# Streaming 64 columns instead of 128 in the TensorE slots of a two-way scan in which one half of the samples takes part

## The chip, the cores and the metric

The kernel runs on one core of a Trainium2 chip. The metric is the device time of that core in microseconds, the median of 3 runs. It runs in float32 throughout.

## The reference

The input `x` has 4 samples of 512 channels, 32 rows and 48 columns. Each sample is first normalised over groups of 16 channels. Then a recurrence goes over the 48 columns, forwards and afterwards backwards over what the forward pass left; the input is added at the end.

```
Wc = conv_w[:, :, 0, 4]                        # 512 x 512, the middle tap of nine
def step(prev, x_i):
    y = einsum('oc,nch->noh', Wc, prev) + conv_b
    y = where(y >= 0, y, prelu_a * y)
    cur = y + x_i
    return (cur, cur)
_, fwd_rest = scan(step, x[0], x[1:])          # over the 48 columns
_, bwd_rest = scan(step, fl[-1], fl[:-1], reverse=True)
x = x + (fwd and bwd result of group_norm(x))
```

Each step needs the one before it: 47 steps forwards and 47 backwards, in each a 512x512 matrix times 512 channels by (samples x 32 rows).

## The kernel before

**Two halves, a few steps apart.** Samples 0 and 1 are half A, samples 2 and 3 are half B. A half has 64 columns (`COLS`: 2 samples x 32 rows) for every one of the 48 positions. Half A starts first, half B follows `SKEW` = 5 steps later, so that its load and its statistics can lie beside the first steps of A. A *slot* is one step of whatever halves take part. There are 99 slots (`LAST`), numbered j: slots 0 to 4 with half A alone (phase "lead"), slots 5 to 93 with both halves ("both forward", "turn", "both backward"), and slots 94 to 98 with half B alone ("drain").

**TensorE, in a slot.** The 512x512 product is 16 units, 4 blocks k of input channels by 4 blocks o of output channels, in the order of the table `UNITS` (L19): tile o=0 is complete with the 9th unit, tile 1 with the 11th, tile 2 with the 13th, tile 3 with the 16th. Each unit is one matmul instruction at L266. Its weights are a 128x128 block of `w_t`. Its moving operand comes from `state`: with both halves `moving` (L138) calls `state_tile`, which takes 2 x 64 columns, one from each half. With one half alone `moving` makes an access pattern with a step of 0 in front, `[0, 2]`, so that the same 64 columns are streamed twice and the matmul writes 128 columns of its PSUM bank. Even slots use banks 0 to 3, odd slots banks 4 to 7.

**What waits for what.** Before the first unit of each k, TensorE waits on `state_ready` for the four-fold count that says that block k of the slot before is final (L265). With the last unit of a tile it raises `tile_done`. ScalarE (L304 to L308) waits for tile o and reads the columns `c` of the halves that take part: twice a Relu, into `above` and, with the sign turned, into `below`. VectorE (or GpSimd, below) adds `above` into `state` (L442), then VectorE adds `below` times the negative slope (L449) and raises `state_ready`; the order within a slot is the table `ORDER` (L22): part 0, whole 0, part 1, part 2, whole 1, whole 2, part 3, whole 3. In the backward phases VectorE then adds the result to the input, in place in `xio` (L461, `add_input`).

**The lead (slots 0 to 4).** GpSimd does the first add (L551), VectorE the second (L476). Between its slots VectorE computes statistics of half B (L363, `stats_b`). ScalarE does those of two of the eight channel blocks of half B (L327 and L330, `pieces`), after its own part of slots 0 to 3. When all are there, VectorE computes means and reciprocal roots (`group_stats`), normalises position 0 of half B (L400, L401) and raises `norm_b`. TensorE, which has meanwhile issued 16 matmuls on the identity (`KEEP_UP`, L275), waits for `norm_b` and then begins slot 5. Earlier, before the last transpose of the weights, it issues 24 of these (`WARM_UP`, L247).

**The drain and the store.** The queue of SyncE stores half A (two transfers of 3 MB) after `out_ready` 1, which VectorE raises at the end of slot 93, and half B (two more) after `out_ready` 2, at the end of slot 98 (L232 to L238). The transfers of half A run while half B is still being computed in the drain.

The lines that the change touches, and those that wait on them:

```
mm = nc.tensor.matmul(psum[:, 4 * par + o, 0:2 * COLS], w_t[:, k, o * P:(o + 1) * P],
                      xs[k], start=k == 0, stop=k == 3)
if k == 3:
    mm.then_inc(tile_done, 1)
```

Of the kernel before, what the change touches and what calls it, by code (L numbers as in the profile page):

```python
# [10 lines left out]
P = 128  # L11
# [19 lines left out]
def scan_program(nc, x, conv_w, conv_b, prelu_a, out):  # L31
# [3 lines left out]
    COLS = NG * H  # L35
# [13 lines left out]
    with ExitStack() as ctx:  # L49
        def sb(name, shape, dt=F32):  # L50
            return ctx.enter_context(nc.sbuf_tensor(name, shape, dt))
# [7 lines left out]
        state = sb("state", [P, 2, W, KT, COLS])  # L59
        w_t = sb("w_t", [P, KT, C])  # L60
# [21 lines left out]
        psum = ctx.enter_context(nc.psum_tensor("psum", [P, 8, 512], F32))  # L82
# [25 lines left out]
        SROW, XROW = 2 * W * FEAT, 2 * KT * COLS * W  # L108
# [9 lines left out]
        def w_raw_block(o, k):  # L118
            t, room = (xio, XHALF) if o < 2 else (state, SHALF)
            base = room + (o % 2) * C * TAPS + k * P * TAPS + MID  # L120
            return bass.AP(t, base, [[SROW, P], [TAPS, P]])
# [5 lines left out]
        def cols(mode):  # L127
            return {"A": slice(0, COLS), "B": slice(COLS, 2 * COLS), "AB": slice(0, 2 * COLS)}[mode]

        def halves(mode, wa, wb, base, step, whole, gap):  # L130

            if mode == "A":
                return wa * step + base, []
            if mode == "B":
                return wb * step + whole + base, []
            return wa * step + base, [[whole + gap * step, 2]]

        def moving(eng, mode, wa, wb, gap, k):  # L138


            if mode == "AB":
                return state_tile(eng, mode, wa, wb, gap, k)
            off, _ = halves(mode, wa, wb, k * COLS, FEAT, SHALF, gap)
            return bass.AP(state, reg(eng, off, 0, SROW - COLS), [[SROW, P], [0, 2], [1, COLS]])

        def reach(half):
            return half[0][0] if half else 0
# [2 lines left out]
        def state_tile(eng, mode, wa, wb, gap, o):  # L150
            off, half = halves(mode, wa, wb, o * COLS, FEAT, SHALF, gap)
            return bass.AP(state, reg(eng, off, 0, SROW - COLS - reach(half)), [[SROW, P]] + half + [[1, COLS]])
# [26 lines left out]
        def positions(j, phase, back=0):  # L179

            fa, ba = j + (1 - back), j * -1 + (STEPS - 1 + back)
            if phase == "lead":
                return "A", fa, None, 0
            if phase == "both forward":
                return "AB", fa, None, -SKEW
            if phase == "turn":
                return "AB", ba, None, fa - SKEW - ba
            if phase == "both backward":
                return "AB", ba, None, SKEW
            return "B", None, ba + SKEW, 0  # L190

        def loop(eng, first, last, body):

            n = (last - first) // UNROLL
            if n > 1:
                with eng.Fori(0, n) as turn:
                    for u in range(UNROLL):
                        body(turn * UNROLL + (first + u), (first + u) % 2)
                first += UNROLL * n
            for j in range(first, last):  # L200
                body(j, j % 2)

        def reg(eng, value, low, high):

            return value if isinstance(value, int) else eng.snap(value, min_val=low, max_val=high)

        def ready(eng, ap):

            eng.lower_ap(ap)
            return ap  # L210

        @block.sync
        def _(sp):
            def load_x(n):
                for t in range(KT):
                    sp.dma_start(xio[:, n // NG, t, (n % NG) * H:(n % NG + 1) * H, :],  # L216
                                 x[n, t * P:(t + 1) * P, :, :]).then_inc(x_loaded[n][t], 16)

            for n in range(NG):
                load_x(n)  # L220
            w_rows = conv_w.rearrange("(o p) i a b -> o p (i a b)", p=P)
            for o in range(KT):
                sp.dma_start(w_raw(o), w_rows[o]).then_inc(w_loaded[o], 16)  # L223
            sp.wait_ge(w_turned, 2)
            for n in range(NG, N):
                load_x(n)

            def store(n):
                sp.dma_start(out[n].rearrange("(t p) h w -> p t h w", p=P),
                             xio[:, n // NG, :, (n % NG) * H:(n % NG + 1) * H, :]).then_inc(stored, 16)  # L230

            sp.wait_ge(out_ready, 1)  # L232
            for n in range(NG):
                store(n)
            sp.wait_ge(out_ready, 2)
            for n in range(NG, N):
                store(n)
            sp.wait_ge(stored, 16 * N)  # L238

        @block.tensor  # L240
        def _(pe):

            pe.wait_ge(ident_done, 2)
            for o in range(KT):
                if o == KT - 1:
                    for _ in range(WARM_UP):
                        nc.tensor.matmul(psum[:, KT, 0:P], ident[:, :], ident[:, :], start=True, stop=True)  # L247
                pe.wait_ge(w_loaded[o], 16)
                for k in range(KT):
                    t = nc.tensor.transpose(psum[:, o, k * P:(k + 1) * P], w_raw_block(o, k), ident[:, :])  # L250
                t.then_inc(w_turned, 1)
            pe.wait_ge(w_ready, KT)
            pe.wait_ge(norm_a, 1)

            def slot(phase):
                def body(j, par):
                    mode, wa, wb, gap = positions(j, phase, back=1)
                    xs = [ready(pe, moving(pe, mode, wa, wb, gap, k)) for k in range(KT)]
                    before = [reg(pe, j * 4 + (k - 3), 1, 4 * LAST) for k in range(KT)]
                    seen = set()  # L260
                    for k, o in UNITS:
                        if k not in seen:
                            seen.add(k)
                            if not (isinstance(j, int) and j == 0):
                                pe.wait_ge(state_ready, before[k])  # L265
                        mm = nc.tensor.matmul(psum[:, 4 * par + o, 0:2 * COLS], w_t[:, k, o * P:(o + 1) * P],  # L266
                                              xs[k], start=k == 0, stop=k == 3)
                        if k == 3:
                            mm.then_inc(tile_done, 1)
                return body  # L270

            slot("lead")(0, 0)
            loop(pe, 1, SKEW, slot("lead"))
            for _ in range(KEEP_UP):
                nc.tensor.matmul(psum[:, 4 * (SKEW % 2), 0:P], ident[:, :], ident[:, :], start=True, stop=True)  # L275
            pe.wait_ge(norm_b, 1)
            slot("both forward")(SKEW, SKEW % 2)
            loop(pe, SKEW + 1, FWD + 1, slot("both forward"))
            for j in range(FWD + 1, FWD + SKEW + 1):
                slot("turn")(j, j % 2)  # L280
            loop(pe, FWD + SKEW + 1, STEPS, slot("both backward"))
            loop(pe, STEPS, LAST, slot("drain"))
# [298 lines left out]
```

## Time and profile before

| | |
|---|---|
| device time, 3 runs | 429.28, 428.53, 429.04 us; median 429.04 |
| span of the profiled execution | 426.3 us |
| median less that span | 2.7 us |
| TensorE (PE) busy | 370.0 us, 87% |
| VectorE (DVE) busy | 329.7 us, 77% |
| ScalarE (ACT) busy | 227.1 us, 53% |
| moved to and from HBM | 34.73 MB |

For the profiled execution the page gives the span, from its first to its last instruction, and no device time of its own; the span is set beside the median here. A row of the page's groups gives the line, the engine, the operation, output<-input, the count, the busy time and the mean of one. PEld is TensorE's weight load. TensorE's records come in twos: the program has 16 matmuls in a slot, the trace 32 records, and 99 slots give the 3168 of L266. The end of a matmul record is modelled, so the spacing of the starts tells more than the length of a record.

### The profile page before, as it was taken

Reading aid. Unit: us, or ns where it says so; the run is one execution under the profiler, and the core shown is the slowest. Engines: PE = TensorE matmul, PEld = TensorE weight load, DVE = VectorE, ACT = ScalarE, POOL = GpSimd, SP = SyncE. Lnnn points to the kernel's source line nnn. Section 1 sums busy time; section 2 is a strip of 40 time slices with the busy share of each in tenths; the row PEclk is TensorE's granted clock in tenths of the full one; section 3 lists DMA queues with packets and bytes.
Section 4 is the critical chain, followed back from the end, with each engine's and each line's share of the span. In section 5 each row is a group of like instructions: output and inputs, shape, how many; then the busy total and the mean of one; then the engine's idle time right before and its main releaser. Section 6 shows DMA issues by size and latency. Waiting matters only on the chain.

```text
span 426.3 us, 10441 instructions
## 1 busy us (share of the span) xinstructions
PE 370.0 (87%) x3264; PEld 367.7 (86%) x3264; DVE 329.7 (77%) x976; ACT 227.1 (53%) x831; POOL 9.2 (2%) x28
## 2 busy tenths in 40 slices
PE   0015989999999999999999999999999999999920
PEld 0015889999999999999999999999999999999920
DVE  3989588999866666666667899999999999999620
ACT  1001594655566666666666666666666666665510
POOL 0000131000000000000000000000000000000000
PEclk9999999999999999999999999999999999999985
DMA  7999920000000000000000000000000000001989
GB/s 262 434 426 420 415 112 2 1 0 0 1 0 0 0 0 0 0 0 0 0 0 2 2 0 0 0 0 0 0 0 0 0 0 0 0 0 43 413 348 379
DMA packets 5674, 34.73 MB, mean 81 GB/s; under 512 B 1056, under 2 KB 1056, under 8 KB 5152
## 3 DMA queue, kind: packets, MB, share of 16 engines
q1 hardware_dynamic: 4992, 34.60, 19.7%
q10 hardware_dynamic: 672, 0.00, 0.1%
q8 instruction: 5, 0.08, 0.1%
q14 instruction: 5, 0.04, 0.0%
HBM read 22.02 MB, written 12.58 MB: 81 GB/s over the span
## 4 chain that ended last, share of the span: by engine, by line
PE 82%; DMA 7%; ACT 3%; DVE 2%; SPq 1%; issue 1%; POOL 0%; DVEq 0%; POOLq 0%
PE psum L266 80%; DMA state<-in_conv_w 7%; PE psum L247 1%; SPq L216 1%; ACT state L327 1%; ACT above L306 1%; ACT below L308 1%; ACT state L330 1%; DVE bstat L363 0%; PE psum L250 0%; SPq L223 0%; DVE chan L366 0%; ACT scaled L333 0%; POOL inv_root L542 0%; DVE state L400 0%
## 5 line engine op out<-in xcount | busy, mean ns | idle before, releaser
L266 PE MATMUL psum<-state,w_t 128*128 (+1 forms) x3168 | 356.2, 275 | 2.9 <-DVE state L476 2.2
L266 PEld LDWEIGHTS psum<-state,w_t 128*128 128x128 f32 x3168 | 354.9, 192 | 4.3 <-DVE state L476 2.0
L306 ACT ACTIVATE above<-psum,bias 128x128 f32<-128x128 f32 (+1 forms) x396 | 145.2, 367 | 139.1 <-PE psum L266 138.4
L442 DVE TENSOR_TENSOR state<-above,state 128x128 f32 (+3 forms) x376 | 106.3, 285 | 54.3 <-ACT above L306 53.1
L308 ACT ACTIVATE below<-psum,neg_bias 128x128 f32<-128x128 f32 (+1 forms) x396 | 145.4, 367 | 0.0
L449 DVE SCALAR_TENSOR_TENSOR state<-below,neg_slope,state 128x128 f32 (+3 forms) x376 | 121.9, 345 | 6.9
L461 DVE TENSOR_TENSOR xio<-xio,state (+2 forms) x54 | 52.8, 978 | 1.8
L391 DVE TENSOR_SCALAR state<-xio,gstat 128x384 f32<-128x384 f32 (+2 forms) x72 | 35.9, 572 | 0.0
L363 DVE BATCH_NORM_STATS2 bstat<-xio 128x6 f32<-128x512 f32 x42 | 26.1, 680 | 8.1 <-DMA xio<-in_x 8.1
L250 PE MATMUL psum<-ident,xio 128*128 128x128 f32 x8 | 2.2, 433 | 30.5 <-DMA xio<-in_conv_w 30.5
L250 PEld LDWEIGHTS psum<-ident,xio 128*128 128x128 f32 x8 | 1.4, 216 | 30.9 <-issue 25.6
L295 ACT COPY w_t<-psum 128x512 f32<-128x512 f32 x4 | 2.3, 586 | 33.8 <-PE psum L250 33.8
L476 DVE SCALAR_TENSOR_TENSOR state<-below,neg_slope,state 128x64 f32<-128x64 f32 x20 | 5.6, 302 | 5.3 <-POOL state L551 5.3
L551 POOL TENSOR_TENSOR state<-above,state 128x64 f32<-128x64 f32 x20 | 7.1, 363 | 32.4 <-ACT above L306 31.7
L247 PEld LDWEIGHTS psum<-ident 128*128 128x128 f32 x48 | 6.6, 225 | 0.0
L247 PE MATMUL psum<-ident 128*128 128x128 f32 x48 | 6.6, 305 | 0.0
L250 PE MATMUL psum<-ident,state 128*128 128x128 f32 x8 | 1.7, 355 | 4.4 <-DMA state<-in_conv_w 4.4
L250 PEld LDWEIGHTS psum<-ident,state 128*128 128x128 f32 x8 | 1.3, 204 | 4.8 <-DMA state<-in_conv_w 4.8
L330 ACT ACTIVATE state<-xio,chan 128x512 f32<-128x512 f32 x6 | 4.4, 738 | 0.1
L327 ACT ACTIVATE state<-xio 128x512 f32<-128x512 f32 x6 | 3.8, 637 | 0.1
L275 PE MATMUL psum<-ident 128*128 128x128 f32 x32 | 3.7, 275 | 0.0
L275 PEld LDWEIGHTS psum<-ident 128*128 128x128 f32 x32 | 3.7, 192 | 0.0
(28 smaller groups left out, 14.6 us busy)
## 6 DMA issues: line engine op xcount, KB each, us to landing
xio<-in_x SPq DMA_DIRECT2D x16, 768.0 KB, 13.6
out_y<-xio SPq DMA_DIRECT2D x4, 3072.0 KB, 13.5
xio<-in_conv_w SPq DMA_DIRECT2D x2, 2304.0 KB, 22.9
state<-in_conv_w SPq DMA_DIRECT2D x2, 2304.0 KB, 33.0
bias<-in_conv_b ACTq DMA_DIRECT2D x1, 2.0 KB, 5.9
slope<-in_prelu_a ACTq DMA_DIRECT2D x1, 0.5 KB, 8.0
```

Source lines behind the costliest of these rows:

```text
L247: nc.tensor.matmul(psum[:, KT, 0:P], ident[:, :], ident[:, :], start=True, stop=True)
L266: mm = nc.tensor.matmul(psum[:, 4 * par + o, 0:2 * COLS], w_t[:, k, o * P:(o + 1) * P], xs[k], start=k == 0, stop=k == 3)
L275: nc.tensor.matmul(psum[:, 4 * (SKEW % 2), 0:P], ident[:, :], ident[:, :], start=True, stop=True)
L306: nc.scalar.activation(above[:, par, o, c], z, ACT.Relu, bias=bias[:, o:o + 1], scale=1.0).then_inc(above_done, 1)
L308: nc.scalar.activation(below[:, par, o, c], z, ACT.Relu, bias=neg_bias[:, o:o + 1], scale=-1.0).then_inc(below_done, 1)
L327: last = nc.scalar.activation(junk, x_piece(1, n, ct, s), ACT.Identity, accum_out=piece_sum[:, 0, s:s + 1])
L330: last = nc.scalar.activation(junk, x_piece(1, n, ct, s), ACT.Square, scale=-1.0, bias=chan[:, 0, b:b + 1], accum_out=piece_sum[:, 1, s:s ...
L363: return nc.vector.bn_stats(bstat[:, b, s, :], x_piece(g, b % NG, b // NG, s))
L391: return nc.vector.tensor_scalar(norm_out(g, b, w0, w1), norm_in(g, b, w0, w1), gstat[:, g, 0, b:b + 1], gstat[:, g, 1, b:b + 1], ALU.subt ...
L442: nc.vector.tensor_tensor(sts[o], split(mode, above[:, par, o, c]), sts[o], ALU.add).then_inc(part_done, 1)
L449: nc.vector.scalar_tensor_tensor(sts[o], split(mode, below[:, par, o, c]), neg_slope[:, 0:1], sts[o], ALU.mult, ALU.add).then_inc(state_re ...
L461: return nc.vector.tensor_tensor(place, place, result, ALU.add)
```

## The change

In slots with one half, `moving` returns an access pattern of 64 columns without the leading repeat, and the matmul writes only the columns of its PSUM bank that belong to the half that takes part, 0 to 63 for A and 64 to 127 for B, as `cols` gives them. With both halves nothing differs (`cols("AB")` is 0 to 127). It is 160 of the 1584 matmul instructions: 80 in slots 0 to 4 and 80 in slots 94 to 98.

```
@@ moving
             if mode == "AB":
                 return state_tile(eng, mode, wa, wb, gap, k)
             off, _ = halves(mode, wa, wb, k * COLS, FEAT, SHALF, gap)
-            return bass.AP(state, reg(eng, off, 0, SROW - COLS), [[SROW, P], [0, 2], [1, COLS]])
+            return bass.AP(state, reg(eng, off, 0, SROW - COLS), [[SROW, P], [1, COLS]])
@@ slot, TensorE
-                        mm = nc.tensor.matmul(psum[:, 4 * par + o, 0:2 * COLS], w_t[:, k, o * P:(o + 1) * P],
+                        mm = nc.tensor.matmul(psum[:, 4 * par + o, cols(mode)], w_t[:, k, o * P:(o + 1) * P],
                                               xs[k], start=k == 0, stop=k == 3)
```

Nothing is moved. On TensorE, slot 0 and the start of the loop over slots 1 to 4 (in the rows, 128x64 is the shape that the matmul writes; ISA and REGISTER_ALU rows compute addresses and counts):

```order
-L266 MATMUL psum<-state,w_t 128x128 x16
+L266 MATMUL psum<-state,w_t 128x64 x16
 L196 UNCONDITIONAL_BRANCH
 L196 ISA
 L209 ISA x2
-L266 MATMUL psum<-state,w_t 128x128 x4
+L266 MATMUL psum<-state,w_t 128x64 x4
 L265 REGISTER_ALU
```

The shape of what is written differs, and no instruction is added, dropped or put elsewhere; the other engines' instructions are the same, in the same order.

## Rows read from the trace of the kernel before

**Rows 1.** The page: engines' busy time, and the chain by engine and line.
```profile
PE 370.0 (87%) x3264; PEld 367.7 (86%) x3264; DVE 329.7 (77%) x976; ACT 227.1 (53%) x831; POOL 9.2 (2%) x28
PE 82%; DMA 7%; ACT 3%; DVE 2%; SPq 1%; issue 1%; POOL 0%; DVEq 0%; POOLq 0%
```

**Rows 2.** The chain that ended last, in time: start us, us, what.
```profile
45.71 3.85 PE psum L266 x32
49.59 0.31 ACT above L306
...
61.24 0.31 ACT above L306
...
62.87 0.42 POOL state L551
...
70.07 0.29 DVE state L476
70.36 0.14 issue
70.49 337.27 PE psum L266 x3008
...
408.73 0.60 DVE xio L461
```

**Rows 3.** Timeline of TensorE, 44 to 75 us: start, length, engine, line, operation, count.
```profile
45.71 7.47 PE L266 MATMUL psum<-state,w_t 128*128 128x128 f32 x64 [0.68 <-ACT w_t L295]
53.67 3.84 PE L266 MATMUL psum<-state,w_t 128*128 x32 [0.49 <-DVE state L476]
...
62.33 3.84 PE L266 MATMUL psum<-state,w_t 128*128 x32 [0.46 <-DVE state L476]
66.01 3.74 PE L275 MATMUL psum<-ident 128*128 128x128 f32 x32
```

**Rows 4.** Timeline of the lead, 45 to 75 us, ScalarE and VectorE.
```profile
48.08 0.31 ACT L306 ACTIVATE above<-psum,bias 128x64 f32<-128x64 f32 x1 [2.42 <-PE psum L266]
48.29 0.31 ACT L308 ACTIVATE below<-psum,neg_bias 128x64 f32<-128x64 f32 x1
...
63.31 0.28 DVE L476 SCALAR_TENSOR_TENSOR state<-below,neg_slope,state 128x64 f32<-128x64 f32 x1 [0.22 <-POOL state L551]
...
64.04 1.81 DVE L363 BATCH_NORM_STATS2 bstat<-xio 128x6 f32<-128x512 f32 x3
...
72.78 0.37 ACT L306 ACTIVATE above<-psum,bias 128x128 f32<-128x128 f32 x1 [5.42 <-PE psum L266]
```

**Rows 5.** Timeline of the drain, 385 to 412 us, all engines.
```profile
392.28 0.23 DVE L442 TENSOR_TENSOR state<-above,state 128x64 f32 x1
...
399.08 0.31 ACT L306 ACTIVATE above<-psum,bias 128x64 f32<-128x64 f32 x1 [1.49 <-PE psum L266]
399.43 0.23 DVE L442 TENSOR_TENSOR state<-above,state 128x64 f32 x1 [0.79 <-ACT above L306]
...
401.26 0.28 DVE L449 SCALAR_TENSOR_TENSOR state<-below,neg_slope,state 128x64 f32 x1
401.58 0.63 DVE L461 TENSOR_TENSOR xio<-xio,state  x1
402.65 0.31 ACT L306 ACTIVATE above<-psum,bias 128x64 f32<-128x64 f32 x1 [1.49 <-PE psum L266]
```

**Rows 6.** By stretch: PE, PEld, DVE, ACT, POOL busy (x), PEclk, DMA share, GB/s.
```profile
57.00:61.00 4.00, 3.48 (x31) 3.29 (x30) 3.21 (x8) 3.90 (x17) 1.46 (x4) 1.00 0.02 6
400.00:407.00 7.00, 7.00 (x65) 7.00 (x64) 4.65 (x18) 3.72 (x17) 0.00 (x0) 1.00 1.02 417
408.00:409.00 1.00, 0.00 (x0) 0.00 (x0) 0.86 (x4) 0.31 (x2) 0.00 (x0) 1.00 0.44 178
409.00:410.00 1.00, 0.00 (x0) 0.00 (x0) 0.33 (x1) 0.00 (x0) 0.00 (x0) 1.00 0.07 31
410.00:411.00 1.00, 0.00 (x0) 0.00 (x0) 0.00 (x0) 0.00 (x0) 0.00 (x0) 1.00 0.81 326
412.00:413.00 1.00, 0.00 (x0) 0.00 (x0) 0.00 (x0) 0.00 (x0) 0.00 (x0) 0.63 1.04 424
413.00:424.00 11.00, 0.00 (x0) 0.00 (x0) 0.00 (x0) 0.00 (x0) 0.00 (x0) 0.50 1.01 416
```

**Rows 7.** TensorE's weight loads and matmuls, a quarter of a microsecond from 37.30.
```profile
37.09 0.69 PE L250 MATMUL psum<-ident,state 128*128 128x128 f32 x2 [4.37 <-DMA state<-in_conv_w]
37.18 0.41 PEld L250 LDWEIGHTS psum<-ident,state 128*128 128x128 f32 x2
```

**Rows 8.** Two stretches of 3.00 us around 40 us, columns as in rows 6.
```profile
37.10:40.10 3.00, 3.00 (x14) 3.00 (x15) 3.00 (x6) 0.59 (x1) 0.00 (x0) 1.00 0.98 418
40.50:43.50 3.00, 3.00 (x29) 3.00 (x28) 1.81 (x4) 0.00 (x0) 0.00 (x0) 1.00 0.94 387
```

More of the change, by code:

```diff
@@ L143, in moving @@
             off, _ = halves(mode, wa, wb, k * COLS, FEAT, SHALF, gap)
-            return bass.AP(state, reg(eng, off, 0, SROW - COLS), [[SROW, P], [0, 2], [1, COLS]])
+            return bass.AP(state, reg(eng, off, 0, SROW - COLS), [[SROW, P], [1, COLS]])
         def reach(half):
@@ L265, in body @@
                                 pe.wait_ge(state_ready, before[k])
-                        mm = nc.tensor.matmul(psum[:, 4 * par + o, 0:2 * COLS], w_t[:, k, o * P:(o + 1) * P],
+                        mm = nc.tensor.matmul(psum[:, 4 * par + o, cols(mode)], w_t[:, k, o * P:(o + 1) * P],
                                               xs[k], start=k == 0, stop=k == 3)
```

## The prediction

> **What bounds the kernel now.** I read the page first, then the chain, then the timelines of the two stretches that the change touches. TensorE is busy 87% of the span and holds 82% of the chain [rows 1]. In time the chain says more [rows 2]: TensorE from 70.49 us for 337.27 us without a break. That is 3008 records, 112.1 ns each, and a slot of 32 records takes 3.59 us. The slots that the change touches lie at both ends of this piece. The lead, slots 0 to 4, runs from 45.71 to 70.49 us and its chain goes over ScalarE, GpSimd and VectorE; the drain, slots 94 to 98, lies in the last 17 us of the piece, and there TensorE sets the pace. Between them nothing is changed, so the middle should move as a block, earlier or later by what the lead gives.
>
> After the last computation (408.73 + 0.60 = 409.33 us [rows 2]) the span goes on for another 17.0 us with stores alone. The drain therefore has two clients: the computation of half B, and the transfers of half A that run beside it.
>
> **The new duration of a matmul.** A record takes 112 ns for 128 columns. Two passes of 128 columns at 2.4 GHz are 107 ns, so I read a record as two passes and little else. The trace has no 64-column matmul. Bounds: from below one half, 56 ns; from above no change, 112 ns. What could keep it from halving is the load of the 128x128 weights, once per record, which becomes no smaller. It is hidden now. How long it takes can be read where the engine was slow. At 37 us, after an idle time of over 4 us, 14 records took 3 us, 214 ns each, and from 40.5 us on 29 took 3 us, 103 ns by the count [rows 8]; I read this as 1.2 GHz and then 2.4 GHz, though the clock column shows 1.00 in both. In the slow stretch the first matmul started at 37.09 us and the second weight load at 37.18 [rows 7], with nothing before it but the first load; so a load takes about 0.1 us at the slow clock. If it follows the array's clock it is about 50 ns at the fast one, less than the 56 of the stream. I take 60 ns, near the lower bound, since the row on the load speaks for it. A slot's TensorE work goes from 3.59 to 1.92 us.
>
> The Trainium skill speaks against this ("TensorE: Matmul & The Clock Gate", section on LDWEIGHTS): it gives the load as the number of weight columns over 1.2 GHz, which is 107 ns for 128 columns, and elsewhere says that the fast load does not apply to float32. By that rule the sum below would be about -0.8 instead of -2.95. Rows 7 agree with its figure at the slow clock, and no row shows it at the fast one.
>
> **Term 1, the lead.** ScalarE is the bound there. It receives the first tile of slot 0 at 48.08 us after waiting 2.42 us [rows 4] and its next idle time in the timeline is the one before slot 5, at 72.78 us [rows 4]: its eight Relus of a slot follow at 0.21 us each (48.08 to 48.29 [rows 4]), then come the statistics of half B, then the next slot. Four later slots of TensorE begin when VectorE has released them and end long before ScalarE comes for them, so halving those saves nothing: their cover is ScalarE's statistics, about 2.6 (4.3 less eight times 0.21) of the 4.3 us from slot to slot. What the chain does hold is slot 0: TensorE 45.71 + 3.85, then ScalarE's `above` of the last tile at 49.59 [rows 2]. TensorE ends slot 0 at 49.56; records there come at 115 ns (3.85 less the 0.28 of the last, over 31). With 60 ns tile 0, 18 records in, is complete 18 x 0.055 = 0.99 us earlier, at 47.09 on ScalarE; the last tile would be 32 x 0.055 = 1.8 us earlier. But ScalarE needs six Relus at 0.21 us before it, so its start is 47.09 + 1.26 = 48.35 rather than 49.59: **-1.24 us**, call it -1.25. Everything behind follows, ScalarE's statistics, the `above` of slot 3 at 61.24, GpSimd at 62.87, VectorE to 70.07, and `norm_b` [rows 2]. The loads of half B are not late for it: from 57 us on they take 2% of the transfer time [rows 6], and VectorE's last statistics, at 64.04 us [rows 4], would begin at 62.8.
>
> At the end of the lead TensorE has less to do. Slot 4 now starts at 62.33 and the 32 records of `KEEP_UP` at 66.01 for 3.74 us [rows 3], which leaves a pause of 0.75 us before slot 5 at 70.49. Afterwards slot 4 would start at about 61.1 and end by 63.4 (it waits for VectorE's last tile, 63.31 + 0.28 less 1.25 [rows 4], before its last 8 units). `KEEP_UP` ends at 67.1 and slot 5 begins at 69.2: a pause of 2.1 us. I count it as nothing, if the clock holds.
>
> **Term 2, the drain.** A slot takes 3.57 us: ScalarE starts tile 0 at 399.08 and at 402.65, each time after 1.49 us of waiting for TensorE [rows 5]. VectorE waits 0.79 us of it. Its own work begins at 399.43 and ends at 401.58 + 0.63 = 402.21, 2.78 us. With 1.92 us on TensorE the cycle is closed by VectorE: from its first add T, the last block is final at T + 2.11 (401.26 + 0.28 less 399.43), TensorE then needs 0.06 us to notice, one unit of 0.12 and about 0.22 for the tail of a matmul and the signal, and ScalarE's `above` comes 0.35 us ahead of VectorE's add (399.08 to 399.43). That is 2.86 us, so a slot takes about 2.8 to 2.9. The first add of the drain, at 392.28, cannot come earlier than the add of slot 93 ahead of it on VectorE allows. Four periods follow: 4 x 0.7 = 2.8 us less until the last output is ready.
>
> The stores cap this. The transfers of half A end in the 408 us slice, those of half B begin in the 410 us slice. In the three slices together 178 + 31 + 326 = 535 of 3 x 417 were moved [rows 6]; what is missing is 1.72 us at full rate. As soon as `out_ready` 2 comes 1.72 us earlier, the second pair of stores is queued behind the first without a gap and the rest of the gain only makes it wait longer. **-1.7 us**, and 1.1 us of the drain's 2.8 are lost to the queue. Any slot time up to 3.14 us gives the same.
>
> **Sum.** -1.25 - 1.7 = -2.95 us: span 426.3 to 423.35, and with the 2.7 us between span and median, 429.04 to 426.1 us. About 0.9 us, 0.2%, is what a measurement here can tell from no change.
>
> **Rivals.** (a) *The weight load binds* at 107 ns, clock-independent. The lead gives 32 x 0.005 = 0.16 us, the drain 4 x (3.57 - 32 x 0.107) = 0.6: 428.2 us. If matmuls don't get shorter at all, 429.0. For it: nothing in the trace shows a load at the fast clock. Against: rows 7. Chance 0.17, which also holds the case that the change does nothing.
>
> (b) *The clock falls once and the gain of the lead is given back.* TensorE would be busy about 2 of every 4.3 us in the lead instead of 3.84, and pause 2.1 us before slot 5. The trace shows the granted clock at 1.00 with pauses of up to 0.75 us, and falling to 0.63 and then 0.50 in the 412 and 413 us slices, over 4 us after the last matmul [rows 2, 6]. Pauses like those to come are not in it. In the lead itself a slow matmul costs nothing (it is back at the old 112 ns or so). In slot 5 it does: the slow stretch at 37 us lasted 3 us [rows 8], and 3 us at half speed lose 1.5. Lead -1.25 + 1.5 = +0.25, drain -1.7 or, if the clock falls there too, -0.6: 427.6 to 428.7 us. Chance 0.18. The Trainium skill bears this out in its section on HAM oscillation in the same page: bursts of matmuls with waits between them can lose the clock again and again. No row here shows that happening.
>
> (c) *The clock stays low into slot 5 and past it: slower.* The place is again the hand-over from `KEEP_UP` to slot 5. A slot of both halves at the slow clock takes 32 x 0.214 = 6.8 us instead of 3.6, and loses 3.2. Then the lead is +2.0 and, with the drain at the slow clock at -0.6, the result +1.4: 430.4 us. It decides from 2 x (1.25 + 0.6) = 3.7 us of slow work in slots 5 and later if the drain gives 0.6, from 5.9 if it gives 1.7. For it: after the change the lead has the least TensorE activity of the program. Against: a slot of both halves is uninterrupted work, and the one rise in the trace took 3 us of it. Chance 0.14.
>
> **How the numbers follow.** The forecast, 426.1, has 0.51; its own range, with the pitch between 56 and 80 ns (at 80 the lead gives 1.0), is 425.5 to 426.7. Rival (a) 0.17, (b) 0.18, (c) 0.14. Faster by over 0.2%: the forecast, most of (b), and little of (a), 0.51 + 0.12 + 0.05 = 0.68. Within 0.2%: the rest of (a) and (b) and a little of (c), 0.19. Slower: 0.13. The range goes from 425.2 to 429.6, which leaves out most of (c) and a tail below.
>
> **What would show it.** Right: records of L266 in the lead at 56 to 65 ns; ScalarE's first tile at 47.1 and slot 5 at 69.2 us; a drain period of 2.8 to 2.9 with VectorE hardly idle; no dip of the transfer rate between the two pairs of stores; PEclk 1.00 throughout. Wrong: a spacing of 107 ns or more (a); a granted clock below 1.00 near 60 to 75 us, with slots of both halves above 3.6 us (b, c). If slot 5 starts early and its slots are at the old pace, but the end is not earlier, the stores were mis-read.

## The result and the profile after

The change makes the kernel slower: 436.81 us, median of 5 runs (436.32 to 442.32), against 429.09 (428.53 to 429.37) for the kernel before beside it; ratio 1.0207, 95% interval 1.0158 to 1.0256. That is +7.7 us where -2.95 was forecast. The profiled execution took 442.32 us, with a span of 440.4, the longest of the five. The ratios of this text leave out executions over 1.5% above the fastest of the same kernel, which here would hide part of the effect itself; where it matters all times are given.

The page after, the granted clock in 40 slices and the chain, against rows 1:

```profile
PE 386.2 (88%) x3264; PEld 384.6 (87%) x3264; DVE 329.7 (75%) x976; ACT 228.7 (52%) x831; POOL 8.6 (2%) x28
PEclk9999755799999999999999999999999999999975
PE 87%; DMA 7%; SPq 1%; DVE 0%; ACT 0%; issue 0%
```

Half the columns in 160 matmuls, and TensorE is busy 16 us longer. The clock row has a dip at slices 5 to 8 that the kernel before hadn't. The chain in time, against rows 2:

```profile
46.85 32.12 PE psum L266 x160
78.97 5.85 PE psum L275 x32
84.83 336.98 PE psum L266 x3008
421.80 0.02 issue
421.82 0.33 ACT above L306
```

Before, the chain left TensorE after slot 0 and went over ScalarE [rows 2]. Now all 160 records of the lead and the 32 on the identity are on it without a break. From the start of slot 0 to that of slot 5 it was 70.49 - 45.71 = 24.8 us; it is 84.83 - 46.85 = 38.0. These 13.2 us are nearly all of the 14.1 us by which the spans differ. The rest, 1.1 us, is slot 0's later start: the identity matmuls before it take 7.5 us here and took 6.4 before. The change doesn't touch these, and I read the difference as one of when the clock rises: before, records came 103 ns apart from 40.5 us on [rows 8], and in the trace after only 6 fall in the microsecond from 40 us and the first 12 in the one from 43. In the traces of this case with 24 of these matmuls they take anywhere from 6.3 us (`drain_32`) to 7.8 (`drain_only`). Behind slot 5 both traces need the same (337.0 and 337.3 us).

By stretch, the clock and the count of records (columns as in rows 6):

```profile
46.85:49.35 2.50, 2.50 (x22) 2.50 (x23) 0.00 (x0) 0.18 (x1) 0.00 (x0) 1.00 1.01 415
50.00:78.00 28.00, 28.00 (x133) 28.00 (x132) 15.54 (x44) 18.59 (x67) 5.42 (x16) 0.50 0.22 92
80.00:85.00 5.00, 5.00 (x32) 5.00 (x31) 2.92 (x12) 0.00 (x0) 0.00 (x0) 0.65 0.00 0
85.00:90.00 5.00, 5.00 (x47) 5.00 (x46) 2.50 (x9) 2.19 (x8) 0.00 (x0) 1.00 0.01 3
405.40:421.50 16.10, 16.10 (x146) 16.10 (x146) 11.10 (x40) 8.97 (x38) 0.00 (x0) 1.00 0.89 363
```

Two things stand here. At the full clock a record of 64 columns comes every 114 ns in slot 0 and every 111 ns in the drain (16.10 over 145 spacings), as one of 128 columns did. And from about 50 us the granted clock is 0.50, the lower level, 1.2 GHz (by single microseconds it is 1.00 up to 49 us, 0.69 in the next and 0.50 after that, so it fell inside slot 0, in which the records follow each other without a pause). A record then takes 28.0/132 = 212 ns, 64 columns or not, a slot 32 of them, 6.8 us, more than the 4.3 that ScalarE set. The clock comes back between 80 and 85 us, when the 128-column matmuls on the identity have begun.

The drain of the kernel after keeps its pace: ScalarE's first tiles, against rows 5, are still 3.57 us apart, each after the same wait of 1.49 us.

```profile
413.12 0.31 ACT L306 ACTIVATE above<-psum,bias 128x64 f32<-128x64 f32 x1 [1.49 <-PE psum L266]
...
416.69 0.31 ACT L306 ACTIVATE above<-psum,bias 128x64 f32<-128x64 f32 x1 [1.49 <-PE psum L266]
```

### The profile page after: what moved, and what is told of

It is laid out like the page before. It is cut to its first block, busy times and chain, and to the rows that moved or that the text cites. A ratio compares the mean times of both kernels' runs of the same rounds, so it can differ in the third digit from the quotient of the medians.

```text
span 440.4 us, 10441 instructions
## 1 busy us (share of the span) xinstructions
PE 386.2 (88%) x3264; PEld 384.6 (87%) x3264; DVE 329.7 (75%) x976; ACT 228.7 (52%) x831; POOL 8.6 (2%) x28
## 4 chain that ended last, share of the span: by engine, by line
PE 87%; DMA 7%; SPq 1%; DVE 0%; ACT 0%; issue 0%
PE psum L266 84%; DMA state<-in_conv_w 7%; PE psum L247 2%; PE psum L275 1%; SPq L216 1%; PE psum L250 0%; SPq L223 0%; DVE xio L461 0%; ACT w_t L295 0%; ACT above L306 0%; DVE state L449 0%; DVE state L442 0%
## 5 line engine op out<-in xcount | busy, mean ns | idle before, releaser
L266 PE MATMUL psum<-state,w_t 128*128 (+2 forms) x3168 | 369.2, 282 | 0.7 <-ACT w_t L295 0.7
L266 PEld LDWEIGHTS psum<-state,w_t 128*128 128x128 f32 x3168 | 368.6, 198 | 1.3 <-ACT w_t L295 0.9
L247 PEld LDWEIGHTS psum<-ident 128*128 128x128 f32 x48 | 7.7, 256 | 0.0
L247 PE MATMUL psum<-ident 128*128 128x128 f32 x48 | 7.7, 337 | 0.0
L275 PE MATMUL psum<-ident 128*128 128x128 f32 x32 | 6.1, 377 | 0.0
L275 PEld LDWEIGHTS psum<-ident 128*128 128x128 f32 x32 | 6.0, 291 | 0.0
```

What stands on the lines that cost most here:

```text
L266: mm = nc.tensor.matmul(psum[:, 4 * par + o, cols(mode)], w_t[:, k, o * P:(o + 1) * P], xs[k], start=k == 0, stop=k == 3)
```

## The experiments

Two theories came from these traces. **W**: a record has a floor set by the 128 columns of its weights, so fewer moving columns save nothing. **C**: streaming half as many columns in the same time loses the full clock in the lead. The rivals are in the expectations.

### The change in one place at a time

```
 lead_only:  if mode == "A": one copy of the 64 columns, else two
 drain_only: if mode == "B": one copy of the 64 columns, else two
 lead_half (slots 0 to 4, tiles o=1 and o=3 only):
-  psum[:, 4 * par + o, 0:2 * COLS], ..., xs[k]
+  psum[:, 4 * par + o, 0:COLS if o % 2 else 2 * COLS], ..., xs[k][o % 2]
```

> 64 columns in the lead (slots 0 to 4) alone; the drain streams them twice as before. Theory C (the clock): with half the columns per record TensorE's granted clock falls in the lead, the lead is then paced by records of 214 ns, and all of the loss is here: ratio to before about 1.018, granted clock 0.50 for 20 to 34 us from about 50 us on. Rival D (the drain or something at the end has a share): clearly less than the whole change, under 1.012. Rival H (the pause before slot 5 is what loses the clock): the clock is 1.00 until about 66 us and 0.50 after it, ratio under 1.01.

Measured: 13 runs, median 437.57 us; 428.44, 428.74 and 432.9, the other ten from 435.6 to 442.6. The 29 runs of before beside it lie within 428.13 to 429.75, and so do the two fastest of this kernel. The ratio of the two medians, of all executions, is 437.57 / 428.83 = 1.020. The profiled one, a span of 440.7 us, has the clock of the change's:

```profile
50.00:80.00 30.00, 30.00 (x143) 30.00 (x143) 17.30 (x50) 19.60 (x70) 7.08 (x21) 0.50 0.21 85
80.00:84.00 4.00, 4.00 (x20) 4.00 (x20) 2.96 (x12) 0.00 (x0) 0.00 (x0) 0.50 0.00 0
84.00:88.00 4.00, 4.00 (x38) 4.00 (x37) 0.36 (x2) 0.87 (x4) 0.00 (x0) 1.00 0.01 4
```

So the lead carries the whole loss, and it is a matter of chance in each execution. Where the clock held (mean 0.984 over the execution, against 0.944 in the profiled one), nothing was gained either: 428.44 is before's own time. Rival H falls for this trace: the clock was at 0.50 from 50 us on, and the matmuls of `KEEP_UP` begin only at 78.8.

> 64 columns in the drain (slots 94 to 98) alone. Theory W (the record of a matmul has a floor that the 128 weight columns set): records stay at 112 ns, a drain slot at 3.57 us, ratio 1.000. My prediction's term 2 would be 0.996 with slots of 2.8 to 2.9 us. Under rival D the ratio is over 1.004. If the clock falls here too, slots of 6.8 us show it.

Measured: 428.99 us, ratio 0.9996 (0.9986 to 1.0007), 12 runs, none above 429.6. The whole drain at the full clock, 146 records in 16 us:

```profile
391.00:407.00 16.00, 16.00 (x146) 16.00 (x145) 11.83 (x43) 8.65 (x36) 0.00 (x0) 1.00 0.78 318
```

Theory W holds, and rival D is out.

> In the lead the output tiles 1 and 3 stream 64 columns once, the tiles 0 and 2 twice: 96 columns per record on average; the drain as before. Theory C: a clock that depends on how much is streamed falls less or not at all here, ratio between 1.000 and that of lead_only. Rival S (any 64-column matmul in the lead does it, by its shape): the same loss as lead_only.

Measured: 428.77 us, ratio 0.9998 (0.9988 to 1.0008), 10 runs, all within 428.03 to 429.56. Half of the lead's matmuls have 64 columns and the clock holds every time, so the shape in itself (rival S) does not lose it.

### What a record costs

```
 after the drain, in the kernel before:
+for m, n in [(128, 64), (128, 256), (128, 32), (128, 128), (64, 128), (64, 64), (32, 32)]:
+    for _ in range(8):
+        matmul(psum[0:m, 4, 0:n], ident[:, 0:m], w_t[:, 0, 0:n], start=True, stop=True)
```

> Before, with 7 groups of 8 matmuls (16 records each) on TensorE behind the drain, where only stores are left. Weights x moving columns: 128x64, 128x256, 128x32, 128x128, 64x128, 64x64, 32x32. Theory W (weights set the floor): 112, about 220, 112, 112, 112 (moving bound), about 60 and under 60 ns per record at the full clock. Rival F (a fixed cost per record, whatever the weights): 112 ns also for 64x64 and 32x32. Rival M (moving columns alone, what I predicted): 60 for 128x64 and 30 for 128x32.

The groups by line of this kernel (busy time, mean of one; in "128*64 128x128" the first pair is the weights, here of 64 columns, the second the 128 moving columns):

```profile
L285 PE MATMUL psum<-w_t,ident 128*128 128x256 f32 x16 | 3.7, 382 | 0.0
L285 PE MATMUL psum<-w_t,ident 128*128 128x128 f32 x16 | 2.0, 280 | 0.0
L285 PE MATMUL psum<-w_t,ident 128*64 128x128 f32 x16 | 2.0, 276 | 0.0
L285 PE MATMUL psum<-w_t,ident 128*128 128x64 f32 x16 | 1.9, 272 | 0.0
L285 PE MATMUL psum<-w_t,ident 128*128 128x32 f32 x16 | 1.9, 271 | 0.0
L285 PE MATMUL psum<-w_t,ident 128*64 128x64 f32 x16 | 1.1, 222 | 0.0
L285 PE MATMUL psum<-w_t,ident 128*32 128x32 f32 x16 | 0.7, 197 | 0.0
```

The records overlap, so the spacing is (busy less one record) over 15. With 128 weight columns it is 0.11 us at 128, 64 and 32 moving columns, and 0.22 at 256. With 64 weight columns it is 0.11 at 128 moving ones and (1.1 - 0.22)/15 = 0.06 at 64; 32 and 32 give 0.03. So in these seven pairs a float32 record's spacing goes with the larger of the two column counts. The 60 ns that I had priced exist, but only if the weights are narrowed as well; a slot would then need twice as many matmuls. The mechanism inside is my reading: loads of weights that run beside the stream of the matmul ahead. The run took 430.95 us with the extra work, one run.

### What keeps and what loses the clock

```
 lead_fill:    lead at 64 columns; behind each of its slots
+  4 x matmul(psum[:, 4 * (1 - par), 0:P], ident[:, :], ident[:, :])      KEEP_UP 16 -> 12
 lead_fill_64: the same with ident[:, 0:COLS] as the moving operand
 slot0_twice:  slot 0 and the drain twice as before, slots 1 to 4 once
 drain_32:     drain streams [[SROW, P], [1, 32]] into 32 columns (sample 3's products left out);
               the rest as before
```

> As lead_only, but behind the 16 matmuls of each slot of the lead 4 more of 128x128 on the identity (8 records, 0.9 us), and 4 fewer in front of slot 5. Theory C (the clock follows how much the array streams): the clock holds, 428.8 us, ratio 1.000, with the lead's own matmuls still at 64 columns. Rival S (64-column matmuls lose the clock by their shape) or a rival by which only the matmuls' own pace counts: 432 to 442 us as in lead_only.

Measured: median 429.39 us over 10 runs, ratio 1.0001 (0.999 to 1.0013); eight within 428.79 to 429.77, two at 436.4 and 436.6. The clock holds mostly, not always. Rival S is out here too: the lead's own matmuls are all at 64 columns.

> As lead_fill, with the fillers behind each slot of the lead at 64 columns too: TensorE has no pause in the lead, and streams 64 columns per record throughout, which is what the drain of drain_only did with the clock at 1.00. Theory P+C (it takes both, half the columns and the pauses): the clock holds in most runs, 429 us, as in the drain. Rival T (in the lead half the columns is too little in itself, and only lead_fill's 128-column fillers helped): 432 to 442 us as in lead_only.

Measured: nine of 11 runs within 429.01 to 429.83, two at 449.3; ratio 1.0002 (0.9992 to 1.0012). In the profiled run, one that held:

```profile
46.00:70.00 24.00, 23.81 (x213) 23.81 (x214) 16.79 (x48) 18.99 (x73) 6.79 (x20) 1.00 0.43 177
```

213 records in 24 us and no pause. Adding *more 64-column matmuls* to the lead mostly saves the clock. But the fillers do two things at once, they close the pauses of 0.5 us per slot and they raise what is streamed in the same time, and no run parts the two. The pauses between slots are not needed for the loss, since in the first profile of the change the clock fell before the first of them. Two runs of 11 lost it even with the fillers, and then 20 us, more than any other kernel here. So half the columns without pauses is no safe place, only a better one. The drain, with the same stream, held in all 12 runs of `drain_only`; 0 of 12 against 2 of 11 can be chance, so these runs don't show that it is safer there.

> Slot 0 and the drain stream twice as before, only slots 1 to 4 stream once. Theory C: the clock falls all the same in most runs, one slot later, and the loss is smaller, 430 to 439 us. Rival Z (slot 0, directly behind the warm-up and its pause of 0.7 us, is what decides): 428.8 us.

Measured: 4 runs, 435.68 to 437.85, median 437.1, ratio 1.0166 (1.0147 to 1.0184). In its profile the first two slots keep the old rhythm and then:

```profile
54.41 20.03 PE L269 MATMUL psum<-state,w_t 128*128 x96 [0.55 <-DVE state L480]
74.22 6.13 PE L279 MATMUL psum<-ident 128*128 128x128 f32 x32
```

Three slots in 20.0 us without a pause, 6.7 each. Rival Z falls: a full slot 0 only postpones the loss.

> In the drain only 32 of the 64 columns are streamed (the products of sample 3 are left out in slots 94 to 98); the lead as before. Theory W: records stay at 112 ns as long as the clock stays. Theory C: with a quarter of the old streaming the clock falls in the drain, slots go from 3.57 to 6.8 us from there on, and the end comes 3 to 10 us later. Rival P (what loses the clock in the lead are the pauses, and a drain without pauses never does): 3.57 us and 428.8 us.

Measured: 441.04 us (439.48 to 442.66, 4 runs), ratio 1.0295 (1.0264 to 1.0325). By stretch:

```profile
390.00:395.00 5.00, 5.00 (x47) 5.00 (x46) 4.55 (x15) 2.55 (x11) 0.00 (x0) 1.00 0.35 138
395.00:400.00 5.00, 5.00 (x27) 5.00 (x26) 2.38 (x10) 2.07 (x8) 0.00 (x0) 0.52 1.01 408
410.00:415.00 5.00, 5.00 (x25) 5.00 (x25) 2.12 (x8) 1.55 (x6) 0.00 (x0) 0.50 0.00 1
```

The drain has no pause and its records follow each other as closely as ever, and still the clock falls to 0.50 at 395 us and stays there. Rival P is out: streaming little is enough, without pauses. At the slow clock a record of 32 columns takes 5.00/24 = 208 ns, as one of 128 does, so the floor follows the array's clock.

### The pause ahead of slot 5

```
-KEEP_UP = 16
+KEEP_UP = 0        # no_keep: in the kernel before; change_no_keep: in the changed one
```

> Before, without the 16 identity matmuls ahead of slot 5: TensorE pauses 4.5 us there. Rival H of my prediction (the pause at the hand-over loses the clock): 430 to 433 us in some runs or all, with slots 5 and on at records of 214 ns for a few us. If one pause of 4.5 us does not lose it, 428.8.

Measured: 431.32 us (431.19 to 431.87, 4 runs), ratio 1.0059 (1.0042 to 1.0076). After a pause of 4.3 us the clock is low:

```profile
68.00:70.00 2.00, 0.00 (x0) 0.00 (x0) 1.10 (x6) 0.30 (x2) 1.31 (x4) 0.82 0.00 0
...
74.00:76.00 2.00, 2.00 (x11) 2.00 (x11) 0.18 (x1) 0.37 (x2) 0.00 (x0) 0.50 0.00 0
76.00:78.00 2.00, 2.00 (x20) 2.00 (x19) 1.64 (x6) 1.88 (x7) 0.00 (x0) 0.98 0.00 0
```

It came back by 76 us, under 5 us into slot 5, and the price was 2.4 us. My rival (b) is thus a real mechanism, though here with a pause of 4.3 us, twice the 2.1 that it was about, and a price of 2.4 us where I gave slot 5 1.5; what a pause of 2.1 us does was not tested. It is not what the change sets off.

> The change without the 16 identity matmuls. In the profile of the change they stand on the path with 5.9 us at the slow clock, and slot 5 begins 4.5 us after its input is ready. Theory K (they cost more than they bring once the clock is lost): 3 to 5 us less than the change in the runs with the longest loss. Theory R (only the 128-column records bring the clock back): slot 5 runs at the slow clock instead, the loss moves there, and the time stays within 2 us of the change.

Measured: 434.77 us median over 11 runs, 430.19 to 439.66. The longest runs are 442.32 - 439.66 = 2.7 us shorter than the longest of the change, a little less than theory K's 3 to 5. Its profile shows both theories at once: slot 5 begins at 75.45 us, soon after its input, and runs at the slow clock until about 79.

```profile
75.45 24.75 PE L266 MATMUL psum<-state,w_t 128*128 128x128 f32 x202 [1.17 <-DVE state L476]
76.00:78.00 2.00, 2.00 (x12) 2.00 (x11) 2.00 (x8) 0.00 (x0) 0.00 (x0) 0.50 0.00 0
```

Once the clock is lost, the 16 matmuls on the identity only stand in the way. Four of the 11 runs took 430.2 to 431.0 us, no more than `no_keep`, and three of these four have its mean clock of 0.974. I read these as runs in which the clock held through the lead and was lost only in the pause; no trace of one was kept.

### The change again, and a faster kernel

> The change itself once more, beside the others on one chip, to see how its time spreads: by theory C it depends on how long the clock stays low, so single runs at 436 and 442 us as already seen, some perhaps at 428.5 as two of lead_only; by a theory of a fixed cost all within 0.3% of 436.8.

Measured: 435.45, 435.7, 436.49 and 442.38 us; ratio 1.015 (1.0132 to 1.0169). The profile of this run shows where the shorter ones come from:

```profile
46.87 7.36 PE L266 MATMUL psum<-state,w_t 128*128 128x64 f32 x64 [0.68 <-ACT w_t L295]
54.77 3.79 PE L266 MATMUL psum<-state,w_t 128*128 x32 [0.54 <-DVE state L476]
59.12 13.58 PE L266 MATMUL psum<-state,w_t 128*128 x64 [0.57 <-DVE state L476]
72.50 5.74 PE L275 MATMUL psum<-ident 128*128 128x128 f32 x32
```

Slots 0 to 2 still have the old rhythm, and only slots 3 and 4 take 13.6 us. In the first profile the clock fell during slot 0. The time depends on when in the lead it falls; none of the nine runs of the change escaped, and two of the 13 of `lead_only` did. The lead is the same in both, and in `change_no_keep`, where by the times about four of 11 escaped, so I take that for chance.

```
-WARM_UP = 24
+WARM_UP = 16       # in the kernel before
```

> Before, with 16 instead of 24 identity matmuls ahead of the last transposes (L247). In the profile of before they take 6.4 us on the chain, while the last block of weights has landed by about 42 us. If the clock holds, slot 0 begins up to 1.8 us earlier and ScalarE's chain with it: 427 to 428 us. If fewer of them leave the clock low at slot 0, the lead is paced by records of 214 ns for a while: 430 to 436.

Measured: 427.33 us (426.97 to 427.91, 4 runs), ratio 0.995 (0.9935 to 0.9965), faster than both kernels. The chain in its trace, against rows 2:

```profile
38.36 5.41 PE psum L247 x32
43.77 0.47 PE psum L250 x4
44.26 0.59 ACT w_t L295
44.90 3.85 PE psum L266 x32
```

Slot 0 begins at 44.90 instead of 45.71 us and slot 5 at 69.67 instead of 70.49. The two traces so explain 0.8 of the 2.1 us between the medians (429.44 beside it); the trace of before (span 426.3) is among its shortest, and the executions beside `warm_16` have spans up to 427.8. Fewer of these matmuls still bring the full clock before slot 0, whose 32 records take 3.85 us in both traces. The lead's 128-column records then hold it.

## Why the prediction was wrong

**The new duration of a matmul: the step that failed.** I took 60 ns for a 64-column record, between bounds of 56 and 112; it measures 111 to 114, the upper bound. The reading that led me there was that of rows 7: the second weight load is shown 0.09 us after the first, at the slow clock, so I halved it for the fast one. The start of a load's record does not say when the load before it was finished. The spacing of many records with few moving columns does, and at the slow clock it is 0.21 us. The rule of the Trainium skill that I had set against the row ("TensorE: Matmul & The Clock Gate", section on LDWEIGHTS) came out right where I had not followed it: its 107 ns for 128 weight columns are near the 112 measured at the full clock. At the slow clock the runs show 0.21 us, which its formula does not give. That rows 7 agree with it at the slow clock, as I had written, rested on the same misreading.

**Term 1, -1.25 us.** The chain was read rightly, but with records of 112 ns there is nothing to gain in slot 0. The fastest runs of `lead_only` (428.44) have before's time.

**Term 2, -1.7 us.** The same. `drain_only` has a ratio of 0.9996 and slots of 3.57 us. Whether the stores would have capped a faster drain was never put to the test. Nor were the small terms of the 2.86 us; the 0.06 us for TensorE to notice is less than the 0.14 that the chain shows between VectorE's end and slot 5's start [rows 2].

**"In the lead itself a slow matmul costs nothing."** This sentence in rival (b) was the second failure, and followed from the first: I took a slow 64-column record to be back at 112 ns. It is 212 ns. A slot then takes 6.8 us, and the lead goes from ScalarE's pace to TensorE's. Therefore (b) and (c) placed the loss behind `KEEP_UP`, in slots of both halves, and priced it at 1.5 to 3.2 us. It lies in the lead, up to 13.2 us of it.

**Rival (c), chance 0.14,** had the right sign and the right cause, too little streamed in the lead. It gave 430.4 us, with the range ending at 429.6; measured 436.81. Its argument against itself, that uninterrupted work brings the clock back, was wrong for this work: 28 us of records in unbroken succession at 64 columns did not bring it back, and 128-column records did within 5 us. The Trainium skill's section on HAM oscillation ("TensorE: Matmul & The Clock Gate") tells of bursts with waits between them. The runs agree with it only for a long wait (`no_keep`, 4.3 us); in the lead the clock fell inside an unbroken slot 0 in the first trace, and afterwards there were no waits any more, because the slow records had filled them.

**Rival (a), chance 0.17,** was right about the record, and would have been the result but for the clock.

## What to carry to other kernels

A float32 matmul against 128 columns of weights cost the same here for 32, 64 or 128 moving columns. Padding a thin one up to 128 is free on that path, and dropping the padding saves nothing. What it can lose is the full clock: before work is taken from TensorE in a stretch where another engine is the bound, look at what the stretch would cost with every record at double its time. Where a kernel's times spread in steps from run to run, read the granted clock of each run first, and the spacing of the records with it: at 37 us the column said 1.00 while they came 214 ns apart [rows 8].

## What the runs showed of the hardware that I had not expected

- In these runs the clock went with what was streamed and not with how busy the trace shows TensorE: at 100% busy it stayed at 0.50 for 28 us with 64 columns, and fell at 100% busy with 32.
- The loss comes by chance: with the same program, 2 of 13 runs (`lead_only`) had none and the others 4 to 14 us; with fillers of 64 columns, 9 of 11 had none and two lost 20 us.
- Half of the lead's matmuls at 64 columns (`lead_half`) was safe in 10 of 10.
- What stays open: what decides in a given run whether, and when, 64 columns lose the clock; whether the pauses between slots have a part in it; and whether the drain (12 of 12 held) is really safer than the lead with fillers (9 of 11).
